# Linear layers as three fp16 products instead of fp32: a two-layer transformer block on one core

## What is computed

```python
qkv = hidden_states @ Wqkv
...
scores = jnp.where(causal[None, None], scores + alibi[None], NEG_INF)
probs = jax.nn.softmax(scores, axis=-1)
attn = jnp.einsum('bhqk,bkd->bqhd', probs, v).reshape(B, S, H)
return attn @ Wo
...
logits = flat @ Wr.T
...
mid = jnp.einsum('tf,erf->ter', flat, A)
all_deltas = jnp.einsum('ter,eor->teo', mid, B) * SCALE
delta = jnp.sum(gates[:, :, None] * all_deltas, axis=1)
...
h = jax.nn.silu(gate) * up
return _dequant_linear(h, down_wq, down_scale)
...
x = x + _L0_attn_ref(xn, L0_attn_Wqkv, L0_attn_Wo) + _L0_ffn_ref(xn, L0_ffn_A, L0_ffn_B, L0_ffn_Wr)
xn = _layernorm(x, axis=-1)
x = x + _L1_attn_ref(xn, L1_attn_Wq, L1_attn_bq, L1_attn_Wk, L1_attn_bk, L1_attn_Wv, L1_attn_bv) + _L1_ffn_ref(xn, L1_ffn_gate_wq, L1_ffn_gate_scale, L1_ffn_up_wq, L1_ffn_up_scale, L1_ffn_down_wq, L1_ffn_down_scale)
```

## Time and profile before

| | us |
|---|---|
| median of 3 runs (667.57 to 668.47) | 668.33 |
| the profiled execution | 666.2 |
| its span on the core, first to last instruction | 664.4 |
| PE busy | 620.2 |
| DVE busy | 454.2 |
| ACT busy | 349.8 |
| POOL busy | 284.2 |

### The profile page before, as it was taken

One profiled execution on the slowest core, in us unless ns is written; L12 is line 12 of the kernel. 1 busy time (PEld: TensorE's weight loads), 2 busy tenths in 40 slices (PEclk: granted clock), 3 DMA queues, 4 the chain that ended last, 5 costly groups with the idle time before them and its releaser, 6 DMA issues.

```text
span 664.4 us, 11736 instructions
## 1 busy us (share of the span) xinstructions
PE 620.2 (93%) x4490; PEld 359.8 (54%) x4490; DVE 454.2 (68%) x936; ACT 349.8 (53%) x603; POOL 284.2 (43%) x299
## 2 busy tenths in 40 slices
PE   5989566978999999999999999999999999999997
PEld 4464444545665565565655755574654555454443
DVE  5775598984988987674668966686796554457422
ACT  3220696682558965843448748852684772023310
POOL 4203476550319773521315826632357561016310
PEclk9998685998999999999999999999999999999999
DMA  9364839466020400321103000401110000000001
GB/s 236 75 111 165 252 67 122 64 91 117 0 83 1 51 1 3 40 44 66 49 33 61 7 3 1 51 33 35 33 33 1 1 1 33 33 33 0 1 16 48
DMA packets 34567, 34.78 MB, mean 52 GB/s; under 512 B 8816, under 2 KB 24080, under 8 KB 34512
## 3 DMA queue, kind: packets, MB, share of 16 engines
q1 hardware_dynamic: 27424, 23.36, 16.6%
q0 software_dynamic: 2672, 8.36, 6.5%
q10 hardware_dynamic: 4416, 2.31, 1.3%
HBM read 30.15 MB, written 8.39 MB: 58 GB/s over the span
## 4 chain that ended last, share of the span: by engine, by line
PE 78%; DVE 8%; ACT 5%; issue 4%; DMA 3%; SPq 1%; POOL 0%; ACTq 0%; DVEq 0%
PE B_bank L1014 28%; PE B_bank L1035 14%; PE A_bank L983 10%; PE A_bank L900 5%; PE B_bank L922 5%; PE A_bank L954 4%; PE E_bank L938 3%; ACT probs L810 2%; DVE mx L1225 2%; ACT e L809 2%; PE A_bank L869 2%; PE B_bank L900 2%; PE E_bank L934 2%; DMA q_parts<-qs 1%; PE B_bank L1004 1%
## 5 line engine op out<-in xcount | busy, mean ns | idle before, releaser
L733 POOL TENSOR_TENSOR probs<-e,probs 128x512 f16<-128x512 f32 x128 | 153.8, 1208 | 189.4 <-ACT probs L810 179.7
L1014 PE MATMUL B_bank<-xs,wgu 128*128 128x512 f16 x896 | 200.5, 379 | 0.0
L809 ACT ACTIVATE e<-E_bank,wn 128x512 f32<-128x512 f32 x192 | 135.6, 706 | 100.1 <-PE E_bank L938 52.5
L1014 PEld LDWEIGHTS B_bank<-xs,wgu 128*128 128x128 f16 x896 | 85.4, 98 | 96.3
L810 ACT ACTIVATE probs<-E_bank,wn 128x512 f16<-128x512 f32 x192 | 135.6, 706 | 0.0
L1035 PE MATMUL B_bank<-wd,hbuf 128*128 128x512 f16 x448 | 100.3, 379 | 0.0
L1225 DVE TENSOR_REDUCE mx<-B_bank 128x8 f32<-128x256 f32 (+6 forms) x168 | 87.5, 584 | 7.2 <-PE B_bank L922 7.1
L745 POOL TENSOR_TENSOR hbuf<-hf,hbuf 128x512 f16<-128x512 f32 x56 | 67.7, 1215 | 43.7 <-ACT hbuf L836 43.6
L983 PE MATMUL A_bank<-wo_sb,attnT 128*128 128x512 f32 x160 | 71.1, 594 | 0.0
L922 PE MATMUL B_bank<-kk,qq 128*128 128x32 f16 (+20 forms) x512 | 67.4, 269 | 3.5 <-DVE mx L1225 3.2
L1035 PEld LDWEIGHTS B_bank<-wd,hbuf 128*128 128x128 f16 x448 | 43.4, 98 | 48.3
(11 more groups left out here) (155 smaller groups left out, 626.0 us busy)
## 6 DMA issues: line engine op xcount, KB each, us to landing
qq<-q_parts SPq DMA_DIRECT2D x21, 256.0 KB
x<-in_x SPq DMA_DIRECT2D x20, 256.0 KB, 4.3
out_y<-x SPq DMA_DIRECT2D x16, 256.0 KB, 2.0
xa<-in_x SPq DMA_DIRECT2D x12, 256.0 KB, 4.9
q_parts<-qs SPq DMA_DIRECT2D x12, 256.0 KB, 3.3
wgu<-in_gate_w POOLq DMA_DIRECT2D x4, 448.0 KB, 5.3
wgu<-in_up_w POOLq DMA_DIRECT2D x4, 448.0 KB, 5.1
wd<-in_down_w POOLq DMA_DIRECT2D x4, 448.0 KB, 7.6
```

The source lines that it names most:

```text
L733: pool.tensor_tensor(probs[:, u % PSLOTS, 1, :], e32[:, w, :], probs[:, u % PSLOTS, 0, :], ALU.subtract).then_inc(s_lo01, 1)
L809: act.activation(e32[:, w, :], psum("exp", i, g, w)[:, :], ACT.Exp, scale=wn[:, 7:8])
L1014: mm = pe.matmul(psum(name, c, i)[:, :].rearrange("p (t n) -> p t n", t=NT), wgu[:, m, k, i * P:(i + 1) * P], xs[:, :, part, k, :], start= ...
```

## The change

Chunk 0 keeps its fp32 products for q and tok. Everywhere else a fp32 operand is a high and a low fp16 part, and the product is high x high + high x low + low x high (`PAIRS`), accumulated in one bank:

- **q** of chunks 1 to 3: 12 fp16 matmuls instead of 4 fp32, in two steps `qa`, `q` of 6; **tok** of chunks 1 to 3: 24 instead of 8; **out** of all batches: 14 fp16 matmuls instead of 5 fp32 (two for LoRA, whose middle lies with both parts in one operand of 128 rows), in two steps `outa` (6) and `out` (8). `half` and `down` become four steps of 8, 6, 8 and 6 matmuls.
- **Operands.** DVE makes the low parts that PE now waits for: of the turned x (step `xT0`, once a tile of chunks 1 to 3) and of the turned attention (step `attT`, twice a batch). The third step of `attT` becomes `midT`, on fp16. `mixb` on DVE writes two parts instead of one (two more instructions a chunk).
- **Weights.** They are loaded as fp32 into `hbuf`, which the feed-forward layer uses later, and split on chip: `squares2` (three ACT instructions), `norm2` on POOL (a second reduction over partitions and two small instructions), `scale2` on DVE (15 instructions of a few elements), ten `hi` steps on POOL (11 instructions) and ten `lo` steps on DVE. q and tok of chunk 1 and the first `out` wait for them. LoRA's matrix is loaded twice; `late` has 12 steps.
- **Order.** `US` has new durations and `RANK` new numbers throughout, so that steps of all engines change places.

```diff
+WS = 256.0
+PAIRS = ((0, 0), (0, 1), (1, 0))
...
+LAST_OF = {"qa": "q", "outa": "out", "half": "down"}
...
-    "PE": {"xT0": (25.5, 4), "tok": (-3.5, -1), "kT": (-12.5, -2), "q": (0.5, 4), "norm": (-25.5, 4), "max": (7, 1), "exp": (7, 2),
...
+    "PE": {"xT0": (51.5, -1), "tok": (14.5, -2), "kT": (-30.5, 1), "qa": (61, 3), "q": (15, 4), "norm": (48, -2), "max": (-27.5, 2),
...
+    for k in range(2):
+        p.add("PE", ("attT", i, k), dve("pv", i, NHG - 1), *([pe("out", i - 1, 1, gap=0.0)] if i else []))
         p.add("ACT", ("attT", i, k), pe("attT", i, k), *([pe("out", i - 1, 1)] if i else []))
+        p.add("DVE", ("attT", i, k), act("attT", i, k))
+    p.add("PE", ("midT", i), dve("mixb", c), *([pe("out", i - 1, 1, gap=0.0)] if i else []))
+    p.add("ACT", ("midT", i), pe("midT", i), *([pe("out", i - 1, 1)] if i else []))
     for t in (0, 1):
-        p.add("PE", ("out", i, t), sp("x1_load", c, 2 * b + t, gap=0.0), act("attT", i, 0), act("attT", i, 1), act("attT", i, 2), pool("late", 3, gap=10.0))
+        p.add("PE", ("outa", i, t), sp("x1_load", c, 2 * b + t, gap=0.0), dve("attT", i, 0), dve("attT", i, 1), act("midT", i),
+              *([dve("lo", 9)] if i == 0 else []))
+        p.add("PE", ("out", i, t), pe("outa", i, t, gap=0.0))
...
+        if c:
+            p.add("DVE", ("xT0", c, t), act("xT0", c, t))
+    turned = dve if c else act
...
+        p.add("PE", ("q", c, m), pe("qa", c, m, gap=0.0))
...
+        p.add("PE", ("half", c, t), pool("up", c, 6), *([pe("up", c, NI - 1, gap=0.0)] if t == 0 else [pe("down", c, t - 1, gap=0.0)]))
+        p.add("PE", ("half2", c, t), pe("half", c, t, gap=0.0))
+        p.add("PE", ("half3", c, t), pe("half2", c, t, gap=0.0), pool("up", c, 10))
+        p.add("PE", ("down", c, t), pe("half3", c, t, gap=0.0), pool("up", c, NI - 1))
...
+            for n in range(3):
+                p.add("ACT", ("squares2", n), *([pool("late", n + 1, gap=6.0), pool("late", 4, gap=6.0)] if n else [act("squares", NK - 1)]))
+            p.add("POOL", ("norm2",), act("squares2", 2))
+            p.add("DVE", ("scale2",), pool("norm2"), dve("scale"))
+            for n in range(10):
+                p.add("POOL", ("hi", n), dve("scale2"), *([pool("clear")] if n == 9 else []))
+                p.add("DVE", ("lo", n), pool("hi", n))
...
+        wq2 = sb("wq2", [P, NK, 2, HID], F16)
+        wtok2 = sb("wtok2", [P, NK, 2, TOKC], F16)
+        wo2 = sb("wo2", [P, NK + 1, 2, HID], F16)
...
+        midz = sb("midz", [P, NT, 2 * NE * LR], F16)
+        attnT = sb("attnT", [P, 2, NK, SEQ], F16)
+        midT = sb("midT", [P, SEQ], F16)
...
+        staged = hbuf[:, :, :, :].rearrange("p a i n -> p (a i n)").bitcast(F32)
+        wq_sb = staged[:, 0:NK * HID].rearrange("p (k n) -> p k n", k=NK)
+        wo_sb = staged[:, NK * HID:(2 * NK + 1) * HID].rearrange("p (k n) -> p k n", k=NK + 1)
+        wtok = staged[:, (2 * NK + 1) * HID:(2 * NK + 1) * HID + NK * TOKC].rearrange("p (k n) -> p k n", k=NK)
...
+            def norm2():
+                pool.wait_ge(s_sq2, 3)
+                pool.partition_all_reduce(wm[:, 0:3], wsq2[:, :], P, bass.bass_isa.ReduceOp.add).then_inc(s_n2b, 1)
+                pool.wait_ge(s_n2b, 1)
+                pool.tensor_scalar(wm[:, 0:3], wm[:, 0:3], 1.0 / NORM ** 2, 1e-30, ALU.mult, ALU.max).then_inc(s_n2c, 1)
+                pool.wait_ge(s_n2c, 1)
+                pool.tensor_tensor(wm[:, 3:6], wm[:, 0:3], mhalf[:, 0:3], ALU.pow).then_inc(s_rn2, 1)
+
+            def hi(n):
+                if n == 0:
+                    pool.wait_ge(s_scale2, 1)
+                if n < NK:
+                    high = pool.tensor_scalar(wq2[:, n, 0, :], wq_sb[:, n, :], wm[:, 15:16], None, ALU.mult)
+                elif n == NK:
+                    pool.tensor_scalar(wtok2[:, :, 0, 0:C_L], wtok[:, :, 0:C_L], wm[:, 15:16], None, ALU.mult)
+                    high = pool.tensor_scalar(wtok2[:, :, 0, C_L:TOKC], wtok[:, :, C_L:TOKC], wm[:, 16:17], None, ALU.mult)
...
+                    col = 10 if n < 2 * NK + 1 else 11
+                    high = pool.tensor_scalar(wo2[:, n - NK - 1, 0, :], wo_sb[:, n - NK - 1, :], wm[:, col:col + 1], None, ALU.mult)
+                high.then_inc(s_whi, 1)
...
+            def squares2(n):
...
+                act.activation(junk, weights, ACT.Square, accum_out=wsq2[:, n:n + 1]).then_inc(s_sq2, 1)
...
-                        mm = pe.matmul(psum("tok", c, w)[:, t * TOKC:(t + 1) * TOKC], xT[:, 2 * w + t, k, :],
-                                       wtok[:, k, :], start=(k == 0), stop=(k == NK - 1))
+                        acc = psum("tok", c, w)[:, t * TOKC:(t + 1) * TOKC]
+                        if c == 0:
+                            mm = pe.matmul(acc, xT[:, 2 * w + t, k, :], wtok[:, k, :], start=(k == 0), stop=(k == NK - 1))
+                        else:
+                            for n, (xpart, wpart) in enumerate(PAIRS):
+                                mm = pe.matmul(acc, xp[:, 2 * w + t, xpart, k, :], wtok2[:, k, wpart, :],
+                                               start=(k == 0 and n == 0), stop=(k == NK - 1 and n == 2))
...
+            def q_tiles(c, m, ks):
+                acc = psum("q", c, m)[:, :].rearrange("p (t n) -> p t n", t=NT)
+                for k in ks:
+                    if c == 0:
+                        mm = pe.matmul(acc, wq_sb[:, k, m * P:(m + 1) * P], xT[:, :, k, :], start=(k == 0), stop=(k == NK - 1))
+                    else:
+                        for n, (wpart, xpart) in enumerate(PAIRS):
+                            mm = pe.matmul(acc, wq2[:, k, wpart, m * P:(m + 1) * P], xp[:, :, xpart, k, :],
+                                           start=(k == 0 and n == 0), stop=(k == NK - 1 and n == 2))
+                return mm
...
+            def qa(c, m):
                 if c == 0:
                     pe.wait_ge(s_wq[m], 16)
+                if c == 1 and m == 0:
+                    pe.wait_ge(s_wlo, NK)
                 if m == 0:
...
-                for k in range(NK):
-                    mm = pe.matmul(psum("q", c, m)[:, :].rearrange("p (t n) -> p t n", t=NT),
-                                   wq_sb[:, k, m * P:(m + 1) * P], xT[:, :, k, :], start=(k == 0), stop=(k == NK - 1))
-                mm.then_inc(full("q", c, m), 1)
+                q_tiles(c, m, (0, 1))
+
+            def q(c, m):
+                q_tiles(c, m, (2, 3)).then_inc(full("q", c, m), 1)
...
+            def turn_mid(i):
+                c, b = i // 2, i % 2
+                wait_free(pe, "midT", i)
+                pe.wait_ge(s_gated, c + 1)
+                for t in range(2):
+                    mm = pe.transpose(psum("midT", i)[:, 0:P].bitcast(F16)[:, t * P:(t + 1) * P], midz[:, 2 * b + t, :], identh[:, :])
+                mm.then_inc(full("midT", i), 1)
+
+            def out_tiles(i, t, ks):
+                for k in ks:
+                    for n, (apart, wpart) in enumerate(PAIRS if k < NK else PAIRS[0:2]):
+                        tokens = attnT[:, apart, k, t * P:(t + 1) * P] if k < NK else midT[:, t * P:(t + 1) * P]
+                        mm = pe.matmul(psum("out", i, t)[:, :], tokens, wo2[:, k, wpart, :],
+                                       start=(k == 0 and n == 0), stop=(k == NK and n == 1))
+                return mm
+
+            def outa(i, t):
+                if i == 0 and t == 0:
+                    pe.wait_ge(s_wlo, 2 * NK + 2)
+                    pe.wait_ge(s_init, 5)
+                if t == 0:
+                    wait_used(pe, "attT", i, 0)
+                    wait_used(pe, "attT", i, 1)
+                    wait_used(pe, "midT", i)
+                wait_free(pe, "out", i, t)
+                out_tiles(i, t, range(2))
+
             def out_(i, t):
-                if i == 0 and t == 0:
-                    pe.wait_ge(s_wo, 32)
-                if t == 0:
-                    for k in range(3):
-                        wait_used(pe, "attT", i, k)
-                wait_free(pe, "out", i, t)
-                for k in range(NK + 1):
-                    mm = pe.matmul(psum("out", i, t)[:, :], attnT[:, k, t * P:(t + 1) * P], wo_sb[:, k, :],
-                                   start=(k == 0), stop=(k == NK))
-                mm.then_inc(full("out", i, t), 1)
+                out_tiles(i, t, range(2, NK + 1)).then_inc(full("out", i, t), 1)
...
             def half(c, t):
-                wait_free(pe, "half", c, t)
-                down_tiles(c, t, range(NI // 2))
+                wait_free(pe, "down", c, t)
...
 
             def down(c, t):
...
+            def lo(n):
+                dve.wait_ge(s_whi, n + 1)
+
+                def low(out, weights, scale, high):
+                    return dve.scalar_tensor_tensor(out=out, in0=weights, scalar=scale, in1=high, op0=ALU.mult, op1=ALU.subtract)
+
+                if n < NK:
...
+            def xT0(c, t):
+                dve.wait_ge(s_xTh, NT * (c - 1) + t + 1)
```

(15 more changed lines are left out.)

239 lines of the change are left out of this document (141 added, 98 removed), and 9 rows, old and new, of tables (RANK, US).

## The result

| | before | after |
|---|---|---|
| median of 8 executions, us | 667.95 | 674.86 |
| the profiled execution's span | 664.4 | 672.0 |
| PE busy | 620.2 | 596.5 |
| PE idle | 44.2 | 75.5 |
| first gate starts at | 190.5 | 201.4 |

The account below looks back on a forecast made before the run. PE was taken to bound the kernel, busy 620.2 of 664.4 us. First gate at 178 plus 468.3 us behind it gave a 646.3 us span; the median lying 3.9 above span, 650 us; range 633 to 662.5.

Parts of the forecast that it names:

- batch 0 takes 33 us from 70 on: Batch 0 behind POOL's first low part: 33 us, to 103, equal to before, with hi at 1.15 us a step.
- PE's prices: fp16 matmuls of 512 columns at 0.216 us each: out 3.02, q 2.59, tok 1.25 us.
- PE busy near 585: PE's busy time over the whole kernel falls by 34.9 us, from 620.2 to 585.3.
- Rival B: Less PE work ahead of the first gate keeps TensorE's clock low: gate at 190, time 662 us, chance 0.17.
- Behind the gate: From the first gate to the end: PE busy 456.6 of 468.3 us.
- The links hide: PE's waits for DVE's low parts of turned x and attention, 28 links, cost 6.3 us in all.
- Rival C: Links don't hide, PE waits for DVE at each of 28: slower, 669 us, chance 0.07.
- First low part at 70: POOL's first low part in the start: at 70 us, range 70 to 76, against 74.86 before.
- Batch 1 in 36 us: The stretch of batch 1: 36 us, to 139, instead of 42, without the maxima of batch 2.
- The rest in 39 us: From batch 1's end to the first gate: 39 us instead of 45.5, the gate starting at 178.

Follow-up runs that it names:

- e2: Kernel before in its own order, q and tok of chunks 1 to 3 and out as fp16 matmuls on constants, no splitting: 648.98 us, ratio 0.9738.
- e11: Changed kernel in its own order, each exp matmul of batches 0 and 1 issued three times: 673.8 us, ratio 1.0077.
- e12: e10 with each exp matmul of batches 0 and 1 issued three times: 658.8 us, ratio 0.9849 to the kernel before.
- e1: Kernel before plus a one-column POOL product right behind the reduction at 26 us, making the change of routine early: ratio 0.9946.
- e4: Changed kernel in its own order, hi and lo steps on 8 columns instead of 512, so weights are not split: ratio 0.9984.
- e5: Changed kernel with the ranks of the kernel before, only hi and lo keeping their new ones: ratio 1.0536.
- e8: Changed kernel in its own order, without norm2's sum over partitions and with hi and lo on 8 columns: ratio 0.9932.
- e13: Changed kernel with both reductions over partitions made by PE and DVE, planned with the changed kernel's durations and ranks: 673.6 us, ratio 1.0112.
- e9: Changed kernel with both reductions made by PE and DVE, replanned with durations from the traces and new ranks: 658.7 us, ratio 0.9889.
- e10: As e9, but hi steps on ACT instead of POOL and an order of its own: 657.1 us, ratio 0.9866.

## Why the prediction was wrong, step by step

In one sentence: the step that failed is "batch 0 takes 33 us from 70 on", with hi at 1.15 us a step and the batch no longer than before. It took 45.1 us from 75.7 on, with hi at 1.6 to 2.1, 17.8 of the 23.4 us by which the first gate is late.

- **PE's prices: right.** A q step is 1.29 + 1.29 = 2.58 us in the chain (forecast 2.59), out 1.29 + 1.73 = 3.02 (3.02), tok 1.08 (1.25). The chain of the changed kernel (start us, us, what):

```profile
327.47 1.08 PE A_bank L955 x24
...
338.73 1.29 PE A_bank L1080 x6
...
342.51 1.73 PE A_bank L1080 x8
...
358.63 1.29 PE A_bank L985 x6
```

- **PE busy near 585: no, 596.5.** Ahead of the gate I expected 154.0 - 14.3 (products) - 11 (max and exp moved behind) = 128.7, and it is 139.0. The other 10.3 I put down to the same instructions at the low level of the clock (granted 0.78 ahead of the gate, 0.87 in e2). A mean fits: the 96 fp16 matmuls of q ahead of the gate take 420 ns each, and in e2 379; but no run parts the 10.3 exactly. e11 and e12, which lift the clock and gain nothing that can be measured, speak for their lying in time in which PE would wait anyway. Rival B's cause fits these rows; its price of 12 us doesn't appear.
- **Behind the gate: right.** 470.6 us against 468.3, with 13.2 idle against 11.7. The links hide: PE's idle time put down to attnT's and x's low parts is 5.2 us in the whole kernel (forecast 6.3). Rival C, the one case in which I let the kernel get slower, named the wrong mechanism.
- **First low part at 70: 75.7,** within my range of 70 to 76. The change to the reduction did go on while the loads flew: POOL was idle 8.65 us for ACT's squares in any case. Two terms were mis-sized. The squares ended at 64.7 and not 61, and the reduction with them, since the loads went out at 54.15, not 51.1, and landed at 62.1. And the change back, which can only begin behind the reduction, took 7.09 us and not 5.3. The 9.45 that I had as the other bound was no price of it either: ACT's first exponential in the kernel before ended at 68.0, so that a part of those 9.45 us was a wait for it, and in e1, with the change back made early, POOL still waits 2.10 us for ACT there. The loads went out late for this reason: in the start of the changed kernel DVE stood in front of chunk 1's norm, which waited for POOL's first change back, and behind it the last q tile of chunk 0:

```profile
38.03 0.55 DVE L1281 TENSOR_SCALAR xa<-x,mv,rs 128x512 f32<-128x512 f32 x1 [2.19 <-POOL rs L781]
39.04 0.55 DVE L1281 TENSOR_SCALAR xa<-x,mv,rs 128x512 f32<-128x512 f32 x1 [0.47 <-POOL rs L781]
39.51 0.87 DVE L1323 SCALAR_TENSOR_TENSOR qs<-B_bank,wn,qs 128x256 f16<-128x256 f32 x2
```

- **Batch 0 in 33 us: 45.1.** Here is half of the miss, 12.1 us, and two steps of mine are wrong. "33 us from 70 on, to 103, where 66 to 103 was the stretch before" took the end of a stretch for the end of a batch: in the kernel before the batch ran from 74.9 to its turn at 110.8, 36 us, with POOL busy 28.6 of them. And POOL's sum, 30 to 33 us, was too small: the hi steps took 18.0 us (8.7 + 7.3 for the nine of 512 columns, and 2.0), not 11.5; the 16 low parts 19.8 (1.24 each), not 18.4; the transfers 2.7, about the 3 I had; and three low parts of batch 1, 3.5 us, were already made before the turn. By the runs, 3 of the 12.1 us are the 36 that the batch took before, 7.2 are the splitting (e4: 37.9 us), and the other 1.9 are open. I had the price of hi from a clearing and a low part, 0.52 and 1.21, as bounds, and the trace says 1.6 to 2.1: the range did not hold it. Most of that is hi's own price: in e5 the fourth hi step, from 80.4 on, takes 1.56 us while DVE does nothing but reduce maxima out of PSUM. A clearing and a low part are other instructions and no bounds for it. The rest, up to 2.1, comes in steps with DVE at work on SBUF.
- **Batch 1 in 36 us: 40.9.** I had taken max of batch 2 out of this stretch, and so it was. The splitting is not the reason for the 4.9 us either, since e4 and e8 need 40.2 and 41.4. DVE is the fullest engine, with 35.2 of 40.9 us, and PE waits for it 2.3, 3.0 and 2.9 us at a time; no run takes this apart, and this part of the miss stays open.
- **The rest in 39 us: 39.7,** right in part by luck. PE is busy only 32.9 us of it and idle 6.8, of which 5.26 stand in front of max of batch 2. I had seen that q of chunk 1 comes "during the exp steps" and did not follow its product on: store, gather, max of batch 2 at 174.6. Batch 1 and the rest together took 79.6 us in the kernel before, with PE busy 72.2; now they take 80.6 with PE busy 60.9. So 11.3 us less of PE's work made the way to the gate no shorter there.

The four terms give 5.7 + 12.1 + 4.9 + 0.7 = 23.4 us, and 178 + 23.4 = 201.4. Of the 26.3 us of span by which the changed kernel stands behind its products alone, e8 gives 12.3 to the splitting and to the sum over partitions. The other 14.0 are not parted by a run of their own. Between e8 and e2, which run the same number of matmuls (4650), they are 8.3 us of PE busy time and 5.7 us of idle time: the links, the order and the clock are in them together. That an order alone can be worth as much is shown by e13 and e9, 12.7 us at equal work.

## What to carry to other kernels

Work taken from the busiest engine counts where that engine is dense (in e2, 19.3 us of PE's work behind the gate gave 16.8 us, and 13.4 us ahead of it gave about 2); the price of what is added must be worked out in the stretch where it lands, on the engines that are fullest there (here POOL and DVE in batch 0, while the page's busy shares speak of PE). Follow a moved step's result on to whoever needs it, through stores and gathers (here 16 to 21 us), and not only to the next step of its engine. A fixed order is part of the kernel like its arithmetic: after a change of durations plan it again with those that the new trace shows, and when a step of one engine is made an experiment, hold the orders of the others fixed.

## What the runs showed of the hardware

- POOL's reduction over partitions costs 5.2 to 5.3 us idle ahead of it (before, e1) and 6.9 to 7.2 behind it, at the next ordinary instruction, even one of one column. Such an instruction right behind it pays this where it costs nothing (e1).
- DVE's instruction on two SBUF tensors of 128x512 (lo) takes 0.7 us with POOL idle and 1.6 beside POOL's low parts (e10), which go from 1.16 to 1.4 us; with one input in PSUM it stays at 0.68 us.
- Lifting TensorE's granted clock from 0.58 to 0.95 by repeated matmuls, in a stretch in which ACT and DVE were busy 33 to 36 of 37 us, brought nothing that could be measured, the repeats' own cost included.
